# Two graph layers and a routed feed-forward: the gate computed inside the second layer, and lots gathered from lists in place of a scatter

## The chip, the cores and the metric

One core of one Trainium2 chip. The metric is the device time of one execution in microseconds (us), the median of several runs. Engines are called as in the profile: PE (TensorE), DVE (VectorE), ACT (ScalarE), POOL (GpSimd), SP (SyncE); "SPq" or "ACTq" is an engine's own sequencer, which issues its DMAs.

## What is computed

6250 nodes with 256 features (49 tiles of 128 rows), 100,000 edges of 8 types whose destinations are crowded at low node numbers.

```python
def rgcn(x, W, Wroot, b):          # W: 8 x 256 x 256
    seg = dst * 8 + etype
    mean = segment_sum(x[src], seg) / max(count(seg), 1)
    return x @ Wroot + b + einsum('nrd,rde->ne', mean, W)

x = x + rgcn(relu(rgcn(layernorm(x), ...)), ...)
z = layernorm(x)
top_w, top_i = top_k(z @ Wg + bg, 2)         # 8 experts, 2 for each node
w = softmax(top_w)
for e in range(8):                 # hidden width 1024
    out += w[:, e] * (gelu(z @ W1[e] + b1[e]) @ W2[e] + b2[e])
return x + out
```

## The kernel before, in words

The program is written engine by engine, with explicit semaphores; nothing is reordered by a tool. It has four stages.

**Setup** sorts edges, normalises x and writes a gather table to DRAM.

**Layers 1 and 2** run over the 49 tiles in the order of `RUNS`, in which runs of tiles with many edges (0 to 12) stand between runs with few. Edge rows come in 792 gathers per layer, each an indirect DMA of 128 rows on POOL (L509) into a ring of 16 slots; SP counts landings and frees slots (L395, L399). A tile is four "couples" (`couple` on PE, k = 0 to 3 in the three `tile_work`). In each, PE multiplies 0/1 selections made by DVE (L1036, and L1044 for every further block) with ring rows (L1384, L1385), ACT and DVE split the means in a high and a low half (L683, L1079), PE turns them (L1400) and, one or two tiles later, makes the 54 products of a tile (L1408). DVE adds the result to `acc` two tiles later (L1053; in layer 1 it is L1050), and takes its statistics (`bn_stats`, L1096). Layer 1 instead counts and inverts in each couple (L1066, L1069) and adds a bias (L1090) and a low half (L1057) in each tile. Layer 2 also reads expert weights for their maximum (ACT loads, L671, DVE L1102).

**The gate stage** begins when all tiles are in `acc`. DVE finishes the statistics of all 49 tiles and normalises tile after tile (`z_rows`, L1155); PE transposes each in f32 (`z_transposes`, L1484), ACT copies it (L745), PE multiplies by the gate matrix (`gate`, L1493). For each chunk of 7 tiles DVE picks the two experts (`choose`, L1169 to L1192), PE ranks (`ranks`, L1499 and L1500), DVE turns ranks into places (`place_rows`), and POOL scatters each tile's rows twice, once per chosen expert, into regions of `lot_in` in DRAM (L533, 98 indirect DMAs of 128 rows). `prepare` converts the weights of an expert (ACT L726, DVE L1217) for experts 0 and 1 inside this stage. At the end DVE works out how many lots each expert has, SP writes zero rows behind each region (L435), waits for all scatters, and loads the first lot (`load_lot`, L441).

**The lots.** A lot is 256 rows of one expert; there are 53. PE multiplies (L1535 up, L1545 down) and transposes the next lot (L1519), ACT applies GELU (L760), DVE splits and combines (`lot`, `take_lot`, `old_tags`, `lot_tags`). POOL gathers the old output rows (`fetch_old`, L545) and scatters the new (`store_new`, L552), then waits until they landed (`landed`, L557).

## Time and profile before

| | before |
|---|---|
| median of 3 runs | 2932.98 us (2931.1 to 2933.84) |
| the profiled execution, first to last instruction | 3487.9 us |
| PE busy | 2472.0 us (71%) |
| DVE, ACT, POOL busy | 1780.8, 1225.2, 1862.5 us |
| DMA | 333.24 MB, mean 96 GB/s |

The profile is of one execution with the hardware profiler on; its span is the only time of that execution that there is. In a row of a group of instructions, "busy, mean ns | idle before, releaser" are the summed time, the mean of one, and the idle time of the engine just ahead of them with what ended it. PE ends are modelled, so a matmul's own duration is longer than the step from one to the next.

### The profile page before, as it was taken

What the parts mean: (1) busy time and instruction counts of PE and PEld (TensorE: products, weight loads), DVE (VectorE), ACT (ScalarE), POOL (GpSimd) and SP (SyncE); (2) the same over time, 40 slices, a digit from 0 to 9 for tenths busy, and PEclk for the clock granted to TensorE, in tenths of its full rate; (3) what the DMA queues carried; (4) which work ended last, traced back from release to release, by engine and by line L of the source; (5) the groups of instructions that cost most, each with busy time, mean ns of one, the idle gap of its engine ahead of it and who ended that gap; (6) DMA issues with size and microseconds to landing.
All of it is one profiled execution on the core that took longest, in us unless ns stands there. A gap on an engine that the chain in (4) does not pass through costs nothing.

```text
span 3487.9 us, 82172 instructions
## 1 busy us (share of the span) xinstructions
PE 2472.0 (71%) x19212; PEld 1832.7 (53%) x19213; DVE 1780.8 (51%) x4984; ACT 1225.2 (35%) x2344; POOL 1862.5 (53%) x1980
## 2 busy tenths in 40 slices
PE   1346787678687786346776587687877428999999
PEld 0113565356365564114564365465656327888887
DVE  7324455345355454124454354354545338787777
ACT  5202343134243342012343143152432126555554
POOL 1666566655655554666556656655563543333333
PEclk9557999589799898557998798798997559999999
DMA  6223323233332232223333333333335234322222
GB/s 216 80 83 112 88 87 91 85 87 89 87 88 87 86 89 64 86 84 97 98 104 97 94 100 99 94 105 95 101 100 163 102 115 132 96 73 71 71 70 59
DMA packets 165489, 333.24 MB, mean 96 GB/s; under 512 B 36078, under 2 KB 102346, under 8 KB 165288
## 3 DMA queue, kind: packets, MB, share of 16 engines
q0 software_dynamic: 91632, 247.48, 24.1%
q1 hardware_dynamic: 39912, 41.03, 4.0%
q10 hardware_dynamic: 33872, 43.92, 3.9%
q8 instruction: 26, 0.43, 0.0%
q14 instruction: 47, 0.39, 0.0%
HBM read 285.39 MB, written 49.07 MB: 96 GB/s over the span
## 4 chain that ended last, share of the span: by engine, by line
PE 44%; issue 22%; DVE 10%; another core or an unknown queue 9%; DVEq 7%; SPq 2%; ACT 2%; DMA 1%; ACTq 0%; POOLq 0%; POOL 0%
PE more_banks L1408 13%; PE sum_banks L1384 9%; PE sum_banks L1385 7%; PE more_banks L1535 4%; PE sum_banks L1535 3%; PE more_banks L1400 3%; PE sum_banks L1545 3%; DVEq L1044 3%; DVEq L1041 2%; DVE sels L1044 2%; DVEq L1027 1%; DVE stage L1079 1%; DVE sels L1036 1%; PE sum_banks L1426 1%
## 5 line engine op out<-in xcount | busy, mean ns | idle before, releaser
L509 POOL DMA_INDIRECT ring<-table,tabs x1584 | 1526.9, 964 | 1046.4 <-SPq L399 670.0
L1384 PE MATMUL sum_banks<-ring,sels 128*128 x2348 | 726.6, 311 | 630.1 <-issue 420.1
L1408 PE MATMUL more_banks<-weights,stage 128*128 128x256 f16 x5292 | 919.1, 290 | 22.0 <-issue 21.4
L1385 PE MATMUL sum_banks<-ring,sels 128*128 x2348 | 732.2, 313 | 41.5 <-issue 38.7
L1384 PEld LDWEIGHTS sum_banks<-ring,sels 128*128 128x128 f16 (+1 forms) x2348 | 242.4, 103 | 928.2 <-issue 896.9
L683 ACT ACTIVATE stage<-sum_banks,inv 128x256 f16<-128x256 f32 x784 | 328.1, 473 | 789.5 <-issue 384.9
L1408 PEld LDWEIGHTS more_banks<-weights,stage 128*128 128x128 f16 x5292 | 531.1, 104 | 135.3 <-issue 37.1
L1036 DVE SCALAR_TENSOR_TENSOR sels<-lane,win_off,tabs 128x256 f16<-128x256 f16 x792 | 349.4, 482 | 422.1 <-remote 181.9
L654 ACT ACTIVATE stage<-more_banks 128x1024 f16<-128x1024 f16 x392 | 402.0, 1026 | 419.1 <-remote 405.6
L1044 DVE TENSOR_SCALAR sels<-lane,win_off,tabs 128x128 f16 x780 | 260.6, 334 | 495.8 <-issue 339.6
L1079 DVE SCALAR_TENSOR_TENSOR stage<-sum_banks,inv,stage 128x256 f16<-128x256 f32 x784 | 347.0, 479 | 57.2 <-issue 40.2
L1385 PEld LDWEIGHTS sum_banks<-ring,sels 128*128 128x128 f16 (+1 forms) x2348 | 241.9, 103 | 116.5 <-issue 68.0
L1400 PE MATMUL more_banks<-ident,stage 128*128 128x128 f16 x3136 | 272.3, 233 | 33.5 <-issue 21.9
L552 POOL DMA_INDIRECT out<-edge_work,lot_ids x106 | 109.2, 1030 | 332.3 <-DVE edge_work L1305 316.2
L681 ACT ACTIVATE stage<-sum_banks 128x256 f16<-128x256 f32 x196 | 75.2, 384 | 546.3 <-issue 231.2
L1400 PEld LDWEIGHTS more_banks<-ident,stage 128*128 128x128 f16 x3136 | 226.3, 105 | 69.9 <-issue 38.2
L1066 DVE TENSOR_SCALAR inv<-sum_banks 128x2 f32 (+1 forms) x196 | 31.1, 159 | 389.3 <-remote 150.1
L1545 PE MATMUL sum_banks<-weights,edge_work 128*128 128x256 f16 x1824 | 208.2, 275 | 8.9 <-DVE edge_work L1289 8.9
L760 ACT ACTIVATE stage<-sum_banks,edge_work,undo 128x256 f32<-128x256 f32 x212 | 117.2, 562 | 239.9 <-PE sum_banks L1535 211.2
L1545 PEld LDWEIGHTS sum_banks<-weights,edge_work 128*128 128x128 f16 x1824 | 179.4, 99 | 31.5 <-issue 9.8
L545 POOL DMA_INDIRECT edge_work<-out,old_ids x106 | 111.4, 1051 | 86.8 <-issue 77.6
L1287 DVE TENSOR_SCALAR edge_work<-stage,scales 128x256 f16<-128x256 f32 x212 | 75.5, 356 | 109.4 <-issue 59.9
(319 smaller groups left out, 2407.5 us busy)
## 6 DMA issues: line engine op xcount, KB each, us to landing
ring<-table,tabs POOLq DMA_INDIRECT x1584
weights<-L_ffn_W ACTq DMA_DIRECT2D x96, 178.5 KB
stage<-L_ffn_W ACTq DMA_DIRECT2D x16, 1024.0 KB, 5.0
edge_work<-lot_in SPq DMA_DIRECT2D x54, 260.0 KB
table<-edge_work ACTq DMA_DIRECT2D x49, 128.0 KB
lot_in<-sels SPq DMA_DIRECT2D x8, 260.0 KB
weights<-L_gnn_W SPq DMA_DIRECT2D x2, 1024.0 KB, 8.3
weights<-L_gnn_W ACTq DMA_DIRECT2D x2, 1024.0 KB
```

Source lines behind the costliest of these rows:

```text
L509: pool.indirect_dma_start(ring_rows[:, b % RING, 0:2 * D], None, tables[layer], bass.IndirectOffsetOnAxis(row_tab[:, b:b + 1], 0)).then_in ...
L654: act.activation(means[:, par, :, :, 2 * k * WIN:(2 * k + 2) * WIN].rearrange("p q r (v n) -> p v (q r) n", v=2), ps_turn[slot].rearrange( ...
L683: act.activation(mean16[:, slot, h, 0:D], ps_sum[slot][h][:, 0:D], ACT.Copy, scale=inv[:, ds(c * 2 + h, 1)]).then_inc(mean_high[layer], 1)
L1036: return v.scalar_tensor_tensor(sel[:, slot, h], lane16[:].unsqueeze(1).to_broadcast([P, 2, P]), win_off[:, ds(w, 1)], key_tab[:, ds((need ...
L1044: v.tensor_scalar(flat(sel_more[:, ds(block & (RING - 1), 1), :]), lane16[:], win_off[:, ds(w, 1)], key_tab[:, ds(block, 1)], ALU.add, ALU ...
L1079: v.scalar_tensor_tensor(mean16[:, slot, h, D:2 * D], ps_sum[slot][h][:, 0:D], inv[:, ds(c * 2 + h, 1)], mean16[:, slot, h, 0:D], ALU.mult ...
L1384: pe.matmul(to[:, 0:D + 1], hot, ring_row[:, ds(at + D, D + 1)], start=first, stop=last, skip_group_check=True)
L1385: return pe.matmul(to[:, 0:D], hot, ring_row[:, ds(at, D)], start=False, stop=last, skip_group_check=True)
L1400: out = [pe.transpose(ps_turn[slot][:, (4 * h + q) * P:(4 * h + q + 1) * P], mean16[:, slot, h, q * P:(q + 1) * P], ident16[:]) for h in r ...
L1408: return [pe.matmul(ps_out[par], rows[:, xp * KD + k, :], w16[:, wp, k, r * D:(r + 1) * D], start=part == PART_ORDER[0] and n == 0, stop=p ...
L1535: ins = pe.matmul(hid_bank[c % 4], up_sb[slot][:, wp, k, c * P:(c + 1) * P], lotT[:, zp, k, :], start=k == 0 and (wp, zp) == PART_PAIRS[0] ...
L1545: ins = pe.matmul(bank[2 + h][:, 0:D], hidT[:, hp, c, h * P:(h + 1) * P], down_sb[slot][:, wp, c, :], start=c == 0 and (hp, wp) == PART_PA ...
```

## The change

**In layer 2** (`gate_tiles` in place of `graph_tiles`: tiles 0 to 3 written out, then the loop by two). After a tile is in `acc`, DVE finishes its statistics by itself (`row_stats`, six small operations); ACT takes the root (`deviation`), DVE inverts (`z_row` on DVE, two operations), ACT normalises the tile into `z_rows` (`z_row` on ACT) and stores it to `z_dram`; a tile later PE transposes it (`z_transposes`, at the start of couple 0), ACT copies (`z_columns`), PE multiplies by the gate (`gate`, at the start of couple 2), and DVE adds the gate's bias (`logit_row`, between the two low halves of couple 2). The last four tiles (`EARLY` = 45 and on) get this behind the layer.

**In the gate stage** `choose` runs once for 45 tiles and once for 4. The scatter is gone. Each of the 12,500 rows has a rank in its expert; its low 7 bits (`low`) and its column 8*(rank // 128) + expert (`high`) become 0/1 rows (`pick_places`, DVE, 14 row sets a chunk), ACT and POOL scale the low ones by the row number in the tile and by the tile's number (`scale_part`, `low_tile`), and 28 f16 matmuls a chunk (`list_rows`) add up, for each place, which node it holds. DVE turns the sums into two tables of row numbers, POOL packs them (16 copies).

**In the lots** POOL gathers each lot's rows from `z_dram` by such a list (`gather_lot`) in place of SP's plain load, and copies the row numbers for its three pairs of indirect DMAs (`take_ids`); DVE's `old_tags` is gone. Zero rows behind the regions and `lot_in` are gone. SP stores `acc` to `out` up to tile position 44 already at the end of the layer. `prepare(1)` stands behind the lists. The core of the diff:

```diff
+                def row_stats(u):
+                    v.wait_ge(layer_done, u + 1)
+                    v.bn_stats(...).then_inc(bn_done, 1)
+                    v.wait_ge(bn_done, u + (TILES + 1))
+                    v.tensor_tensor(flat(mv[:, ds(u, 1), :]), ...)
+                    v.tensor_tensor(apart, ...).then_inc(mean_ready, 1)
+                    v.wait_ge(mean_ready, u * 2 + 1)
+                    v.tensor_scalar(mean, mean, 0.5, None, ALU.mult)
+                    v.scalar_tensor_tensor(apart, ...).then_inc(mean_ready, 1)
+                    v.wait_ge(mean_ready, u * 2 + 2)
+                    v.scalar_tensor_tensor(spread, ...).then_inc(var_ready, 1)
...
-                            if k == 3 and age == 2:
-                                v.wait_ge(layer_done, t - 1)
-                                v.bn_stats(flat(bn[:, ds(t - 2, 1), :]), flat(acc[:, ds(t - 2, 1), :])).then_inc(bn_done, 1)
+                            if k == 1 and age >= 3:
+                                z_row(t - 3, 1 - par, age >= 4)
+                            if k == 3 and age >= 2:
+                                row_stats(t - 2)
...
+                            if k == 0 and age >= 3:
+                                deviation(t - 3)
+                            if k == 0 and age >= 4:
+                                z_columns(t - 4, par, 1 - par)
+                            if k == 2 and age >= 3:
+                                z_row(t - 3, 1 - par, age >= 4)
...
+                    if layer == 1 and k == 0 and age >= 4:
+                        z_transposes(t - 4, par, 1 - par, t - 2)
                     regs, at, need, end = load_couple(c)
+                    if layer == 1 and k == 2 and age >= 4:
+                        gate(t - 4, par, ps_sum[slot][1][:, GATE_AT:GATE_AT + X])
...
-            for c in range(CHUNKS):
-                pool.wait_ge(zs_ready, c + 1)
-                for i in range(CHUNK):
...
-                    for k in range(2):
-                        pool.indirect_dma_start(lot_in, ...)
+            for c in range(CHUNKS):
+                pool.wait_ge(places_marked, 2 * c + 1)
+                if c >= 2:
+                    pool.wait_ge(listed, c - 1)
+                pool.tensor_tensor(low_tile[c % 2]..., low_hot[c % 2]..., node_tile..., ALU.mult).then_inc(tile_scaled, 1)
...
+            def pick_places(c):
+                if c >= 2:
+                    v.wait_ge(listed, c - 1)
+                    v.wait_ge(part_scaled, c - 1)
+                    v.wait_ge(tile_scaled, c - 1)
...
+                v.scalar_tensor_tensor(low_hot[c % 2], lane16..., 0.0, low, ALU.add, ALU.is_equal).then_inc(places_marked, 1)
+                v.scalar_tensor_tensor(high_hot(c), col_no..., 0.0, high, ALU.add, ALU.is_equal).then_inc(places_marked, 1)
...
-                sp.dma_start(lot_rows, lot_in[ds(row, LOT), :].rearrange("(h p) d -> p h d", p=P)).then_inc(lot_loaded, 16)
+                for h in range(HALVES):
+                    pool.indirect_dma_start(lot_rows[:, h, :], None, z_dram, bass.IndirectOffsetOnAxis(next_ids[:, h:h + 1], 0)).then_inc(lot_loaded, 16)
```

PE at a tile's end and the start of the next one in layer 2's loop (L1384 and L1385, now L1555 and L1556, multiply ring rows; L1408, now L1592, is a product). Before:

```order
L1400 MATMUL more_banks<-ident,stage 128x128 x8
L336 REGISTER_ALU
L336 COMPARE_AND_BRANCH
L1376 TENSOR_LOAD pe_row
L1433 REGISTER_ALU
L1384 ISA
L1384 MATMUL sum_banks<-ring,sels 128x257
```

Now:

```order
L1584 MATMUL more_banks<-ident,stage 128x128 x8
L392 REGISTER_ALU
L392 COMPARE_AND_BRANCH
L1573 MATMUL more_banks<-ident,weights 128x128 x2
L1547 TENSOR_LOAD pe_row
L1621 REGISTER_ALU
L1555 ISA
L1555 MATMUL sum_banks<-ring,sels 128x257
```

The two f32 transposes of a normalised tile (`z_rows` lies in `weights`) stand ahead of couple 0's first sums, and two f32 gate products stand in the same way ahead of couple 2's.

DVE behind the last two additions to `acc`. Before (L1155 then normalises 14 tiles):

```order
L1143 BN_STATS stage<-acc 128x6 x2
L820 TENSOR_TENSOR mv<-stage 128x49
L821 TENSOR_TENSOR stage<-stage 128x49
L822 TENSOR_TENSOR mv<-stage 128x49
L823 TENSOR_TENSOR stage<-stage 128x49
```

Now, at the far end of the stage, with the last three chunks' places (L1352 low, L1354 high), the tables, and expert 1's `prepare`:

```order
L1369 SCALAR_TENSOR_TENSOR weights<-stage,scales,weights 128x512 x8
L1352 SCALAR_TENSOR_TENSOR sels<-lane,edge_work 128x1792
L1354 SCALAR_TENSOR_TENSOR ring<-sels,edge_work 128x3920
L1352 SCALAR_TENSOR_TENSOR stage<-lane,edge_work 128x1792
L1354 SCALAR_TENSOR_TENSOR edge_work<-sels,edge_work 128x4704
L1352 SCALAR_TENSOR_TENSOR sels<-lane,edge_work 128x1792
L1354 SCALAR_TENSOR_TENSOR ring<-sels,edge_work 128x5488
L1430 TENSOR_SCALAR edge_work<-more_banks 128x400
L1431 TENSOR_SCALAR edge_work<-more_banks 128x400
L1432 SCALAR_TENSOR_TENSOR edge_work<-more_banks,edge_work 128x400
```

The 49 normalisations left DVE, and 14 wide operations, of 1792 and of 784 to 5488 elements, came to it.

POOL in the loop over an expert's lots. Before:

```order
L566 ISA
L552 DMA out<-edge_work,lot_ids 6250x256 x2
L542 ISA
L545 DMA edge_work<-out,old_ids 128x256 x2
L556 ISA
```

Now:

```order
L639 ISA
L593 ISA
L593 COPY next_ids<-edge_work 128x2
L594 ISA
L600 DMA edge_work<-z_dram,next_ids 128x260 x2
L593 ISA
L593 COPY out_ids<-edge_work 128x2
L594 REGISTER_ALU
L622 REGISTER_ALU
L625 DMA out<-edge_work,out_ids 6250x256 x2
L593 ISA
L593 COPY old_ids<-edge_work 128x2
```

The gather for the lot after the next and its copy stand ahead of the store.

## Rows read from the trace of the kernel before

**Rows 1.** Stretches: start:end, us; busy PE, PEld, DVE, ACT, POOL; PEclk, DMA, GB/s

```profile
112.00:1387.00 1275.00, 897.78 (x6762) 620.71 (x6762) 590.16 (x1726) 399.40 (x736) 748.10 (x777) 0.82 0.30 87
1387.00:2665.00 1278.00, 893.50 (x6760) 620.37 (x6760) 550.06 (x1369) 385.97 (x687) 764.25 (x798) 0.83 0.33 96
2665.00:2862.00 197.00, 71.19 (x330) 64.88 (x330) 76.41 (x320) 32.38 (x77) 99.43 (x108) 0.51 0.43 144
2862.00:3488.00 626.00, 594.11 (x5299) 518.17 (x5296) 476.88 (x1320) 336.50 (x736) 220.62 (x212) 0.98 0.27 81
2481.00:2551.00 70.00, 64.32 (x628) 53.65 (x626) 42.93 (x105) 38.89 (x72) 40.57 (x43) 1.00 0.38 108
```

**Rows 2.** DVE's tile results in layers 1 and 2: durations, first and last start

```profile
L1050 DVE SCALAR_TENSOR_TENSOR stage<-more_banks,gnn_undo,bias_bc x49: 472/475/484, 336.6 to 1382.7; 128x256 f32 x47, 128x256 f32<-128x256 f32 x2
L1053 DVE SCALAR_TENSOR_TENSOR acc<-more_banks,gnn_undo,acc x49: 473/475/485, 1626.8 to 2664.9; 128x256 f32 x46, 128x256 f32<-128x256 f32 x3
```

**Rows 3.** Gate stage, PE in order of time: start, duration

```profile
2664.84 0.27 PE L1479 MATMUL more_banks<-ident,edge_work 64*128 64x64 f32 x1
...
2672.34 0.67 PE L1484 MATMUL more_banks<-ident,ring 128*128 128x128 f32 x2
2672.80 0.86 PE L1493 MATMUL sum_banks<-edge_work,sels 128*128 128x8 f32 x4
2673.51 0.67 PE L1484 MATMUL more_banks<-ident,ring 128*128 128x128 f32 x2
...
2725.03 1.02 PE L1493 MATMUL sum_banks<-edge_work,sels 128*128 128x8 f32 x4 [9.69 <-issue]
...
2858.74 1.12 PE L1519 MATMUL more_banks<-ident,edge_work 128*128 128x128 f32 x4 [34.18 <-DMA edge_work<-lot_in]
2861.45 0.82 PE L1535 MATMUL sum_banks<-edge_work,weights 128*128 128x256 f16 x3 [1.59 <-DVE edge_work L1269]
```

**Rows 4.** Gate stage, POOL's scatters in order of time: two neighbours

```profile
2791.83 0.97 POOL L533 DMA_INDIRECT lot_in<-ring,edge_work  x1 [0.30 <-issue]
2793.11 0.97 POOL L533 DMA_INDIRECT lot_in<-ring,edge_work  x1 [0.30 <-issue]
```

**Rows 5.** DVE lines: min/median/max ns, first and last start

```profile
L1217 DVE SCALAR_TENSOR_TENSOR weights<-stage,scales,weights x48: 740/743/752, 2752.0 to 3056.9; 128x512 f16<-128x512 f32 x48
L954 DVE SCALAR_TENSOR_TENSOR weights<-weights,gnn_scale x2: 5000/5006/5011, 257.1 to 1550.2; 128x4608 f16<-128x4608 f32 x2
```

**Rows 6.** DVE in order of time: the scan, the scales, the lots' numbers

```profile
95.48 1.78 DVE L996 TENSOR_TENSOR_SCAN stage<-ones,stage 1x784 f32<-1x784 f32 x1
...
2675.38 1.07 DVE L1222 TENSOR_REDUCE most<-edge_work 128x4 f32<-128x512 f32 x1 [0.99 <-DMA edge_work<-most_dram]
...
2832.05 0.16 DVE L1242 SCALAR_TENSOR_TENSOR edge_work<-expert_no,edge_work 128x8 f32<-128x8 f32 x1
...
2834.47 0.48 DVE L1256 MEMSET edge_work<- 128x512 f32 x1 [0.29 <-DVE lot_meta L1254]
```

**Rows 7.** Setup, PE in order of time: seven 392-column f16 matmuls

```profile
77.35 2.47 PE L1350 MATMUL more_banks<-weights,ones 112*128 112x392 f16 x7 [5.57 <-DVE weights L914]
```

**Rows 8.** Groups by line: a POOL memset, ACT's copy, DVE's smallest operation

```profile
L499 POOL MEMSET stage<- 128x784 f32 x1 | 0.8, 757 | 20.5 <-DVEq L894 20.5
L745 ACT ACTIVATE sels<-more_banks 128x256 f32<-128x256 f32 x49 | 18.5, 382 | 104.8 <-remote 52.2 <-PE more_banks L1484 28.0 <-issue 19.9
L1066 DVE TENSOR_SCALAR inv<-sum_banks 128x2 f32 (+1 forms) x196 | 31.1, 159 | 389.3 <-remote 150.1
```

**Rows 9.** A lot in the last stage: POOL, then PE, each by time

```profile
3271.78 1.03 POOL L545 DMA_INDIRECT edge_work<-out,old_ids  x1 [0.30 <-DMA out<-edge_work,lot_ids]
3279.12 1.02 POOL L552 DMA_INDIRECT out<-edge_work,lot_ids  x1 [6.32 <-DVE edge_work L1305]
...
3270.68 0.60 PE L1519 MATMUL more_banks<-ident,edge_work 128*128 128x128 f32 x4
3271.12 5.40 PE L1545 MATMUL sum_banks<-weights,edge_work 128*128 128x256 f16 x48
```

675 lines of the change are left out of this document (419 added, 256 removed).

## The prediction

> **What bounds the kernel now.** I first cut the span at the three places where the work changes and read the stretches [rows 1]. Both layers take 1275 to 1278 us, the gate stage 197 us, the lots 626 us. In the lots PE works 594 of 626 us with a granted clock of 0.98: they are bound by PE. In the gate stage no engine is busy for more than half of the time (POOL 99 of 197 us, DVE 76, PE 71 at clock 0.51, the lower level of 1.2 GHz): it is a chain of waits. In order of time it runs from the end of layer 2 at 2664.8 to the first product of a lot at 2861.5, 196.6 us [rows 3]. POOL issues its scatters at best 1.28 us apart [rows 4], so 98 of them are 125 us. What lies around them is the lead to the first scatter, POOL's waits for places, the zero rows and the first load: PE waits 34.2 us for that load at the end.
>
> In layer 2 a stretch of five tiles with few edges takes 70 us, 14 us a tile, with PE busy 64.3 us at full clock, DVE 42.9 and ACT 38.9 [rows 1]. There PE is the bound. In tiles with many edges the mean is longer and PE idles, since POOL's gathers (764 of 1278 us busy) and their landings set the pace. DVE has room: from the first to the last tile result layer 1 takes 1046.1 us and layer 2 1038.1 us [rows 2], though DVE is busy for 40 us more in layer 1, 0.8 us a tile [rows 1], with a count and a reciprocal ahead of each couple's selections. Most of a microsecond of DVE time per tile thus costs next to nothing.
>
> **The gate stage, rebuilt from rows.** From here every time counts from the end of layer 2. DVE is the chain for the most part, so I add up its list. The unit: 512 elements take 0.743 us and 4608 take 5.006 us [rows 5], so an operation takes 0.21 us and 1.04 ns an element. The smallest is 0.16 us [rows 8], 0.25 with a link to the next.
> - The last-but-one tile's root stands on ACT behind a copy that waits for PE's transposes, which stand behind the layer's products: 1.5 us until DVE is free (0.46 for two transposes [rows 3], 0.38 for the copy [rows 8], the root and DVE's two operations).
> - `choose` for 45 tiles: 12 operations of 360 elements at 0.585 us, a scan of 400 at 1.78/784 us an element [rows 6], some small ones and the links: 10.1 us.
> - Last tile's result, statistics, maxima, `z_row`: 3.3 us. `place_rows` for 45 tiles: 4.9 us. `choose` and `place_rows` for 4 tiles, 23 small operations and a scan: 7.0 us. Logits and weights: 2.7 us.
> - Scales: 1.07 us and eight small ones, 2.4 us. The lots' numbers: 2.4 us (2832.05 to 2834.47) [rows 6]. `prepare(0)`: 8 x 0.67 = 5.4 us at the step of [rows 5].
> - `pick_places`: seven times 1792 elements at 2.08 us, and 784 to 5488 elements, 24.3 us: 38.9 us.
>
> That is 78.6 us of DVE. Behind it: the last 28 matmuls of 392 columns. Seven such take 2.47 us [rows 7], which is the step at the lower level of the clock, where this stage runs now [rows 1]: 9.9 us. Three DVE operations of 400 elements before the last table, 1.9 us. POOL's 16 copies of 50 numbers, 0.25 us each, 4.1 us with the first list (no row has such a copy; the ends are 0.1 and 1 us each, and the memset of 784 elements in 0.757 us [rows 8] is nearest). The first gather: two issues at 1.35 us and a landing of 2.2 us, 4.8 us. Transposes and `take_lot` up to the first product: 2.7 us (2858.74 to 2861.45) [rows 3]. The sum is 102 us. The trace has stalls in this stage that no dependency explains, one of 9.69 us on PE [rows 3]; straight code is as long as before, and I add one of 8 us. So 110 in place of 196.6: **minus 87 us** (ends: minus 105 without stalls and with the last matmuls at full clock; minus 50 with three stalls and copies of 1 us).
>
> What is free beside it: ACT's scaling of 1792 elements stands beside DVE's wide operations; the waits in `pick_places` from the third chunk on look two chunks back. Expert 0's weights are loaded from the moment the last tile is done and used 45 us later. `prepare(1)` (5.4 us) runs while POOL packs. The stores of `out` up to position 44 moved on SP from this stage to the end of layer 2, where nothing is queued behind them. The tags that SP writes to `z_dram` are needed only 50 us later.
>
> **Layer 2.** For 45 tiles PE gets two transposes and a gate product in two parts. In the gate stage a tile's step is 0.46 us from transposes to products and 0.71 us on to the next [rows 3], 1.17 us at the lower clock; four f32 transposes take 0.44 us at full clock in the lots (3270.68 to 3271.12) [rows 9]. So at full clock 0.22 and half of 0.71: 0.58 us a tile. 45 x 0.58 = **plus 26 us**. Tiles that wait for gathers hide theirs, which I leave as margin. DVE gets seven or eight small operations, about 1.7 us with their links; ACT a root, a copy of 0.38 us, a normalisation and a DMA issue, about 1.7 us. Against 14 us a tile that makes DVE 10.3 and ACT 9.5 us: hidden, as the two layers' equal pace shows [rows 2]. If the cover goes, it is because they stand in the chain of a couple (below). Ends: plus 10 and plus 90 us.
>
> **The lots.** PE's lot is unchanged, 626/53 = 11.8 us on the mean [rows 1]. POOL gets two more indirect DMAs and three copies, 3.5 us, in a queue that idles 6.3 us in each lot [rows 9]. The new gather stands ahead of the store but asks only for a lot that PE takes one and a half lots later. DVE loses three small operations. Zero, with ends of minus 5 and plus 20 us (one wait more at each of the 8 experts).
>
> **Sum:** 3487.9 - 87 + 26 = 3427 us for a profiled execution. The median of the timed runs is 2933 us, 555 us below that span. The lots cannot be what shrinks (PE is full there), and POOL's steps in the gate stage are long work of its own; the layers, with a register or branch instruction at every turn, are the likely place. So I carry the difference over unchanged: 2933 - 61 = **2872 us**. If the whole span shrank alike (0.84), it would be 2933 - 51 = 2882.
>
> **Rivals.**
> 1. *POOL and DVE block each other in the gate stage.* POOL's seven products of 1792 elements run exactly beside DVE's wide operations. If only one of them can run at a time, the products join DVE's chain. No row has a two-input operation on POOL. By the memset (0.97 ns an element, twice for two inputs [rows 8]) they are 7 x 3.4 = 24 us: 2872 + 24 = 2896. For it: nothing hides them then. Against it: no row shows a DVE operation stretched beside POOL's DMAs, though these do not read as much.
> The Trainium skill, page "SBUF — State Buffer", section "SBUF: two separate sides", says that the port pair that both use is "an exclusive lock, not a bandwidth split", for DVE operations with two SBUF inputs against a GpSimd operation that reads SBUF. That is this case, and speaks against the change; no run here shows it yet. The Trainium skill's "GPSIMD Engine Reference", section 3.1, has 4497 ns for a `tensor_tensor` of 2048 elements; as an estimate that is 3.9 us for 1792, so 27 us in place of 24.
> 2. *Couples wait for the new steps.* PE's gate product at couple 2 waits for ACT's copy, which stands behind the means and the root of couple 0; DVE's couples 2 and 3 now carry result, maxima, logits and statistics in a row. If a tile loses 1.6 us instead of 0.58: plus 72 instead of 26, 2918.
> 3. *The same to a full degree, and slower than before.* If each tile loses the time of most of a couple (14/4 = 3.5 us), say 2.5 us, the cost is 45 x 2.5 = 112 us: 2933 - 87 + 112 = 2958. It decides from 87/45 = 1.9 us a tile. Against it: DVE and ACT have a third of the time free, and every hand-over is one to two couples ahead of its use.
> 4. *Layer 2 hides PE's part too* because the timed execution is nearer to POOL's pace (792 gathers at the step of [rows 4] are 1014 us, against 1278) than the profiled one: 2846.
> 5. *The change does not do what it says*, in that lists still end late: POOL's copies or the first gather wait for the tags or for `z_dram`. Priced within the end of minus 50: 2909.
>
> **How the numbers follow.** The forecast has a chance of 0.42, rival 1 0.2, rival 2 0.13, rival 3 0.08, rival 4 0.1, rival 5 0.07. The likeliest gives 2872. The range: from rival 4 less some margin for the sum, 2835, to beyond rival 2, 2930; rival 3 and a little on each side are left out. A measurement of this kernel can tell about 0.2% from no change, 6 us. Below 2927 lie all cases but rival 3 and the upper edge of rival 2: faster 0.87, within 0.2% 0.04, slower 0.09.
>
> **What would show it right or wrong.** Right: the stretch from the last product of layer 2 to the first of a lot is about 110 us, DVE is busy in most of it, with L1352 at 2.1 us and L1354 from 1.0 to 5.9 us; light tiles take 14.6 us with PE still full; POOL idles some 3 us in each lot. Wrong: DVE rows stretched or late behind POOL's L576 (rival 1); PE waiting in front of L1579 or L1573, or light tiles above 15.5 us (rivals 2 and 3); PE waiting at lots for the gather.

## The result and the profile after

The changed kernel takes 3134.05 us (median of 4 runs, 3131.12 to 3140.09), the kernel before 2933.41 us (2931.1 to 2936.35): a ratio of 1.0685, 95% interval 1.067 to 1.07. It is 201 us slower; forecast were 61 us less.

One thing must be known before the traces are compared. The execution that the prediction was read from spans 3487.9 us; a second profile of the same, unchanged kernel spans 2930.4 us, like its timed runs, and the changed kernel's spans 3133.2. I therefore compare with the second profile. That the first one's excess is no property of the kernel is what the run before_again was for:

> The kernel before, unchanged, for a profile that can be laid beside the one after: that one's span is within 0.1% of its timed median, while the first profile of the kernel before is 555 us above its own. Theory A: the excess lay in POOL's gathers of the tiles with many edges, in both layers alike; this profile then has a span of about 2933 us, the heaviest tile takes about 46 us in place of 70, and light tiles stay at 14 us. Theory B: the excess is part of every profile of this kernel; then the span is 3488 us again.

Measured: 2933.21 us, ratio 1.0001 (0.9991 to 1.0011). The span of 2930.4 us is theory A's; its account of where the excess lay holds only in part. The heaviest tile takes 46.2 us in layer 1, as expected, but 57.4 in layer 2; tiles with few edges did not stay at 14 us but take 12.2 in layer 2; and of the excess of 557 us, some 50 lie ahead of layer 1's first result, 50 between the two layers, 36 in the gate stage and 12 in the lots, next to 407 in the two layers.

The windows by stage of this second profile of before are, in this order, from 1200 us (between the two layers) to the last product of layer 2, the gate stage up to the first product of a lot, the lots, and five tiles with few edges. The columns are busy time of each engine, granted clock, DMA share, GB/s:

```profile
core 0: us, PE busy (x) PEld busy (x) DVE busy (x) ACT busy (x) POOL busy (x), PEclk, DMA share, GB/s
1200.00:2156.00 956.00, 791.44 (x6661) 584.54 (x6659) 531.14 (x1322) 375.56 (x687) 718.91 (x747) 0.91 0.41 121
2156.00:2316.00 160.00, 67.52 (x328) 65.06 (x327) 76.61 (x319) 32.49 (x77) 98.55 (x108) 0.52 0.54 181
2316.00:2930.40 614.40, 588.01 (x5300) 519.17 (x5300) 478.32 (x1321) 325.52 (x736) 219.46 (x212) 0.98 0.27 82
2003.09:2064.19 61.10, 60.54 (x620) 52.84 (x619) 42.29 (x103) 37.98 (x71) 46.47 (x49) 1.00 0.45 132
```

The same three stretches of the changed kernel, columns as above:

```profile
1200.00:2289.50 1089.50, 848.81 (x6934) 635.29 (x6934) 578.06 (x1703) 417.95 (x827) 717.53 (x762) 0.88 0.41 119
2289.50:2416.10 126.60, 42.60 (x236) 28.38 (x235) 88.52 (x140) 28.18 (x36) 54.30 (x27) 0.60 0.23 62
2416.10:3133.20 717.10, 613.28 (x5300) 529.06 (x5300) 474.03 (x1161) 325.05 (x736) 362.08 (x476) 0.96 0.24 72
```

| from .. to | before, us | after, us | difference | forecast |
|---|---|---|---|---|
| first tile result to last product of layer 2 | 1325.0 to 2155.8: 830.8 | 1326.2 to 2289.4: 963.2 | +132.4 | +26 |
| gate stage | 160.2 | 126.7 | -33.5 | -87 |
| lots | 614.4 | 717.1 | +102.7 | 0 |

With the 1.2 us at the start that is +202.8, the difference of the two spans. The gate stage did get shorter. Both stretches around it, which I had taken as nearly free, got longer by over 100 us each. From the page of after, the busy times and one of the two queues that fetch instructions:

```profile
PE 2375.4 (76%) x19390; PEld 1800.6 (57%) x19391; DVE 1836.6 (59%) x5025; ACT 1229.7 (39%) x2443; POOL 1961.9 (63%) x2177
...
q14 instruction: 153, 1.25, 0.1%
```

and the same lines of the second profile of before:

```profile
PE 2318.1 (79%) x19212; PEld 1775.9 (61%) x19213; DVE 1782.6 (61%) x4984; ACT 1192.1 (41%) x2344; POOL 1865.3 (64%) x1980
...
q14 instruction: 47, 0.39, 0.0%
```

PE and VectorE are busy for only 57 and 54 us more, so most of the 202 us are waits on them. POOL is busy for 97 us more, and in the lots for 143 (362.1 against 219.5, last rows of the windows). The other line to see is that of queue q14, which fetches code: 153 packets of 8 KB in place of 47.

**Layer 2.** From result to result, tiles with few edges alternate between 14 to 17 and 19 to 22 us. The five that end between 2105.6 and 2191.2 take 85.6 us; the same five take 61.1 in before (the last row of its windows above), 12.2 each. VectorE between two of them:

```profile
2069.83 0.42 DVE L1194 BATCH_NORM_STATS2 stage<-acc  x1
...
2071.16 0.16 DVE L1204 SCALAR_TENSOR_TENSOR mv<-stage,mv  x1
2076.28 0.49 DVE L1169 SCALAR_TENSOR_TENSOR sels<-lane,win_off,tabs 128x256 f16<-128x256 f16 x1 [4.97 <-issue]
```

After the last small operation of a tile it does nothing for 4.97 us and waits for nobody ("issue"), at the point where its loop of two tiles jumps back. The DMA queues in the stretch 2072 to 2079 us show code arriving just then:

```profile
q14 instruction: 3, 0.02, 1.0%
```

Not all of the 4.97 us is the wait for code. VectorE's own sequencer takes the branch at the jump back (L392) at 2071.3 us and its next instruction at 2074.3:

```profile
L392 DVEq COMPARE_BRANCH  x1: 72/72/72, 2071.3 to 2071.3; - x1
L392 DVEq FUSED_REGOPS  x1: 105/105/105, 2074.3 to 2074.3; - x1
```

That step out of the branch takes 2.98 us at the median of the 21 jumps back, and 0.28 in code_moved_40 below, which executes the same loop. The other 1.9 us are a register load and address work, which stand at every tile's start.

Over the layer, the waits of VectorE for "issue" and of PE for VectorE:

```profile
DVE sels L1169 <- issue: 150.1, 57, 5.5
...
PE sum_banks L1555 <- DVE sels L1177: 102.4, 66, 5.3
```

and in before:

```profile
DVE sels L1036 <- issue: 14.4, 16, 1.5
```

where PE waits for VectorE (L1384 for L1044) for 60.0 us, 81 times.

**The lots.** Most lots take 12.7 to 13.2 us, in before 10.9. PE waits for the gathered rows 48 times:

```profile
PE more_banks L1714 <- DMA edge_work<-z_dram,next_ids: 87.8, 48, 4.5
```

One round of POOL in after, all its records:

```profile
2708.21 0.18 POOL L593 COPY next_ids<-edge_work 128x2 int32 x1 [2.58 <-issue]
2709.24 0.96 POOL L600 DMA_INDIRECT edge_work<-z_dram,next_ids  x1 [0.85 <-POOL next_ids L593]
2710.51 0.99 POOL L600 DMA_INDIRECT edge_work<-z_dram,next_ids  x1 [0.31 <-issue]
2711.51 0.19 POOL L593 COPY out_ids<-edge_work 128x2 int32 x1
2712.71 1.02 POOL L625 DMA_INDIRECT out<-edge_work,out_ids  x1 [1.01 <-issue]
2714.04 1.00 POOL L625 DMA_INDIRECT out<-edge_work,out_ids  x1 [0.30 <-issue]
2715.02 0.22 POOL L593 COPY old_ids<-edge_work 128x2 int32 x1
2716.10 0.98 POOL L618 DMA_INDIRECT edge_work<-out,old_ids  x1 [0.86 <-POOL old_ids L593]
2717.39 0.98 POOL L618 DMA_INDIRECT edge_work<-out,old_ids  x1 [0.30 <-issue]
2720.97 0.18 POOL L593 COPY next_ids<-edge_work 128x2 int32 x1 [2.61 <-issue]
```

and in before, where POOL's idle time [rows 9] is also 5.94 us a lot:

```profile
2707.29 1.01 POOL L552 DMA_INDIRECT out<-edge_work,lot_ids  x1 [5.94 <-DVE edge_work L1305]
2708.61 1.00 POOL L552 DMA_INDIRECT out<-edge_work,lot_ids  x1 [0.31 <-issue]
2709.91 1.04 POOL L545 DMA_INDIRECT edge_work<-out,old_ids  x1 [0.31 <-issue]
2711.26 1.02 POOL L545 DMA_INDIRECT edge_work<-out,old_ids  x1 [0.30 <-DMA out<-edge_work,lot_ids]
2718.22 1.01 POOL L552 DMA_INDIRECT out<-edge_work,lot_ids  x1 [5.94 <-DVE edge_work L1305]
```

In after POOL waits for no other engine in the whole round. It lasts 2708.21 to 2720.97 = 12.76 us, and that is the lot's length.

**The gate stage.** Of POOL's seven products the first two and the last three, in the timeline of POOL:

```profile
2311.75 3.83 POOL L576 TENSOR_TENSOR edge_work<-sels 128x1792 f16<-128x1792 f16 x1 [27.48 <-DVE sels L1352]
2323.35 4.66 POOL L576 TENSOR_TENSOR edge_work<-stage,sels 128x1792 f16<-128x1792 f16 x1 [7.76 <-DVE stage L1352]
...
2357.47 14.01 POOL L576 TENSOR_TENSOR edge_work<-sels 128x1792 f16<-128x1792 f16 x1 [9.04 <-DVE sels L1352]
2371.44 3.17 POOL L576 TENSOR_TENSOR edge_work<-stage,sels 128x1792 f16<-128x1792 f16 x1
2379.70 8.74 POOL L576 TENSOR_TENSOR edge_work<-sels 128x1792 f16<-128x1792 f16 x1 [5.09 <-DVE sels L1352]
```

and six of VectorE's operations beside them:

```profile
2311.58 0.97 DVE L1354 SCALAR_TENSOR_TENSOR ring<-sels,edge_work 128x784 f16<-128x784 f16 x1
...
2312.69 2.94 DVE L1359 TENSOR_SCALAR edge_work<-edge_work 128x45 f32<-128x45 f32 x1
...
2325.45 2.58 DVE L1335 CAST edge_work<-edge_work 128x8 int32<-128x8 f32 x1
...
2357.31 4.23 DVE L1354 SCALAR_TENSOR_TENSOR ring<-sels,edge_work 128x3920 f16<-128x3920 f16 x1
2361.46 2.01 DVE L1352 SCALAR_TENSOR_TENSOR stage<-lane,edge_work 128x1792 f16<-128x1792 f16 x1
2363.39 5.05 DVE L1354 SCALAR_TENSOR_TENSOR edge_work<-sels,edge_work 128x4704 f16<-128x4704 f16 x1
```

L1354 ends 0.80 us after the first product has begun (2312.55 against 2311.75), and 3.83 - 0.80 = 3.0 us are left. For the second it is 4.66 - 1.61 = 3.0, for the third and fourth (5.48 and 6.29 us long) and for the last (8.74 - 5.71) the same 3.0. The fifth takes 14.01 us: until 2368.44 VectorE's three wide operations run back to back, and 3.0 us later it ends. The sixth runs with VectorE idle, in 3.17. The other way round, the addition of a constant to 45 elements takes 2.94 us and a cast of 8 elements 2.58 us, and both end as the product does; so do another such cast (2.95 us) and another addition (3.14 us).

### The profile page after: what moved, and what is told of

It is laid out like the page before. It is cut to its first block, busy times and chain, and to the rows that moved or that the text cites. A ratio compares the mean times of both kernels' runs of the same rounds, so it can differ in the third digit from the quotient of the medians.

```text
span 3133.2 us, 83695 instructions
## 1 busy us (share of the span) xinstructions
PE 2375.4 (76%) x19390; PEld 1800.6 (57%) x19391; DVE 1836.6 (59%) x5025; ACT 1229.7 (39%) x2443; POOL 1961.9 (63%) x2177
## 4 chain that ended last, share of the span: by engine, by line
issue 27%; PE 24%; POOL 22%; DVE 8%; DVEq 6%; DMA 6%; POOLq 4%; SPq 0%; ACT 0%; ACTq 0%
POOL ring L547 16%; PE more_banks L1592 9%; PE sum_banks L1555 6%; PE sum_banks L1556 4%; DMA ring<-table,tabs 3%; PE more_banks L1584 3%; DVEq L1160 3%; POOLq L631 3%; DMA out<-edge_work,out_ids 2%; POOL edge_work L600 2%; POOL out L625 2%; DVE stage L1241 1%; POOL edge_work L576 1%; DVE sels L1169 1%; DVEq L1177 1%
## 5 line engine op out<-in xcount | busy, mean ns | idle before, releaser
L1555 PE MATMUL sum_banks<-ring,sels 128*128 x2348 | 699.7, 299 | 422.9 <-DVE sels L1177 269.2
L1592 PE MATMUL more_banks<-weights,stage 128*128 128x256 f16 x5292 | 878.1, 281 | 0.6
L1556 PE MATMUL sum_banks<-ring,sels 128*128 x2348 | 704.5, 301 | 0.0
L1555 PEld LDWEIGHTS sum_banks<-ring,sels 128*128 128x128 f16 (+1 forms) x2348 | 235.2, 100 | 700.0 <-issue 672.6
L1592 PEld LDWEIGHTS more_banks<-weights,stage 128*128 128x128 f16 x5292 | 514.0, 101 | 100.7 <-issue 12.4
L1177 DVE TENSOR_SCALAR sels<-lane,win_off,tabs 128x128 f16 x780 | 267.5, 343 | 387.9 <-SPq L451 318.7
L1584 PE MATMUL more_banks<-ident,stage 128*128 128x128 f16 x3136 | 257.3, 229 | 37.9 <-DVE stage L1241 37.8
L1556 PEld LDWEIGHTS sum_banks<-ring,sels 128*128 128x128 f16 (+1 forms) x2348 | 235.6, 100 | 48.8 <-issue 3.1
L1740 PE MATMUL sum_banks<-weights,edge_work 128*128 128x256 f16 x1824 | 219.4, 284 | 0.0
L625 POOL DMA_INDIRECT out<-edge_work,out_ids x106 | 110.3, 1040 | 82.8 <-issue 57.6
L600 POOL DMA_INDIRECT edge_work<-z_dram,next_ids x108 | 111.4, 1032 | 62.7 <-POOL next_ids L593 46.2
```

Source lines behind the costliest of these rows:

```text
L600: pool.indirect_dma_start(lot_rows[:, h, :], None, z_dram, bass.IndirectOffsetOnAxis(next_ids[:, h:h + 1], 0)).then_inc(lot_loaded, 16)
L1177: v.tensor_scalar(flat(sel_more[:, ds(block & (RING - 1), 1), :]), lane16[:], win_off[:, ds(w, 1)], key_tab[:, ds(block, 1)], ALU.add, ALU ...
L1555: pe.matmul(to[:, 0:D + 1], hot, ring_row[:, ds(at + D, D + 1)], start=first, stop=last, skip_group_check=True)
L1556: return pe.matmul(to[:, 0:D], hot, ring_row[:, ds(at, D)], start=False, stop=last, skip_group_check=True)
L1584: out = [pe.transpose(ps_turn[slot][:, (4 * h + q) * P:(4 * h + q + 1) * P], mean16[:, slot, h, q * P:(q + 1) * P], ident16[:]) for h in r ...
L1592: return [pe.matmul(ps_out[par], rows[:, xp * KD + k, :], w16[:, wp, k, r * D:(r + 1) * D], start=part == PART_ORDER[0] and n == 0, stop=p ...
```

## The experiments

The times are medians; the ratio is to the kernel before on the same chip, with its 95% interval. "Layer", "gate" and "lots" are differences to the second profile of before in the three stretches of the table, read from each run's own profile.

| run | us | ratio (95%) | layer | gate | lots | code packets |
|---|---|---|---|---|---|---|
| after | 3134.05 | 1.0685 (1.067, 1.07) | +132.4 | -33.5 | +102.7 | 153 |
| one_tile_loop | 3054.96 | 1.0409 (1.0392, 1.0426) | +54.6 | -35.0 | +103.8 | 45 |
| ids_together | 3068.26 | 1.0457 (1.044, 1.0474) | +134.0 | -35.0 | +39.7 | 153 |
| both_mended | 2988.72 | 1.0187 (1.017, 1.0204) | +54.1 | -35.4 | +38.8 | 46 |
| before_unused_code | 2935.03 | 1.0004 (0.9995, 1.0014) | -0.7 | -0.3 | +3.1 | 48 |
| before_one_tile_loop | 2933.98 | 1.0001 (0.9992, 1.0011) | +0.4 | +0.3 | -0.4 | 46 |
| products_on_act | 3108.39 | 1.0599 (1.0581, 1.0617) | +131.2 | -54.9 | +95.2 | 154 |
| all_four | 2955.36 | 1.0077 (1.006, 1.0094) | +53.5 | -53.5 | +15.7 | 46 |
| code_moved_40 | 3031.32 | 1.0331 (1.0313, 1.0348) | +30.9 | -33.3 | +101.3 | 48 |
| code_moved_128 | 3126.97 | 1.0661 (1.0643, 1.0679) | +124.7 | -32.9 | +103.9 | 154 |
| before_unused_moved_90 | 2981.73 | 1.0164 (1.0147, 1.0181) | +47.8 | -1.2 | +1.3 | 159 |
| stats_spread | 2906.86 | 0.9911 (0.9895, 0.9928) | +10.8 | -54.9 | +13.6 | 46 |
| two_tiles_placed | 2905.51 | 0.9907 (0.9891, 0.9924) | +5.6 | -54.8 | +14.4 | 49 |

Two kernels that execute the same work as before, before_unused_code and before_one_tile_loop, differ from it by up to 3.1 us in a stage: so much lies within one profile's noise.

### Layer 2: the code of VectorE's loop

one_tile_loop takes one tile a turn:

```diff
-            with eng.Fori(2, PAIRS) as i:
-                body(i * 2, 0, 4)
-                body(i * 2 + 1, 1, 4)
+            with eng.Fori(4, TILES) as t:
+                body(t, t & 1, 4)
```

> The changed kernel, with VectorE's loop of layer 2 written with one tile a turn in place of two (the same instructions run, in the same order; some 170 in the loop in place of some 330). Theory A (the loop's code has become too long to stay with the engine, so each turn waits for code at the jump back, 5.0 us, and once more inside, up to 1.7 us): every second tile loses its extra 5 to 6 us, 22 turns, so 110 to 145 us less than 3134: 2990 to 3024 us, and the packets of the instruction queue fall from 153 to about 50. Theory B (the couples wait for the new steps, rivals 2 and 3 of the prediction): nothing changes, 3134 us within 10.

Measured: 79 us less, all of it in the layer, and the code packets are gone: theory A, though 31 us less than its lower end. The alternation is gone too; behind the first heavy tiles a tile with few edges now takes 14 to 17 us. Two controls on the kernel before followed. before_one_tile_loop writes its layer-2 loop in the same form:

> The kernel before, with VectorE's loop of layer 2 written with one tile a turn, as in one_tile_loop. It tells what that form costs by itself. Theory A (the form costs nothing, since the old loop of 298 instructions stayed with the engine): 2933 us within 6, and the 51 us that one_tile_loop's layer 2 is longer than the one before are all the price of the added steps. Theory B (a jump back at each tile costs 1 to 2 us of VectorE, which light tiles can't hide): 2933 + 20 to 45 us, and the added steps cost that much less.

Measured: no difference. before_unused_code puts unexecuted code into each tile of its loop:

```diff
                             if k == 3 and age == 2:
+                                with v.If(end[0] > 30000):
+                                    for _ in range(16):
+                                        v.memset(most[:, 3:4], 0.0)
                                 v.wait_ge(layer_done, t - 1)
```

> The kernel before, with 16 small instructions and a branch over them in each of the two tiles of VectorE's loop of layer 2: the branch always skips them, so what is executed grows by one untaken or taken branch a tile, and the loop's code from some 298 to some 334 instructions, which is its length in the changed kernel. Theory A (length of the loop's code): every second tile of layer 2 takes 5 us more, 22 turns: 2933 + 80 to 130 = 3013 to 3063 us, with about 150 packets on the instruction queue in place of 47. Theory B (executed work alone costs): 2933 to 2938 us and 47 packets.

Measured: 2935 us and 48 packets, a miss. Length alone is not it. I had also counted from a listing of the program; the compiled one has, without labels, 281 instructions in the loop of before (from the 977th on), 315 with the unused code, 321 in the changed kernel (from the 1208th on). That left two theories: a limit between 315 and 321, or the place of the loop's ends in blocks of code. The next three runs put code that is never executed ahead of the loop, which moves the loop and nothing else:

```diff
                 regs, need, end = load_meta(0, 4)
+                if layer == 1:
+                    with v.If(end[0] > 30000):
+                        for _ in range(38):
+                            v.memset(most[:, 3:4], 0.0)
```

> The changed kernel with 38 small instructions and a branch over them ahead of VectorE's loop of layer 2, never executed: the loop's 321 compiled instructions (labels not counted) begin at the 1247th in place of the 1208th. before_unused_code showed that 315 instructions from the 977th on cost nothing. Theory A (code is kept in blocks, and what counts is how many blocks the loop touches; both earlier results together leave only offsets at which a move by 40 brings the 321 into one block fewer): the stall of 5 us at the jump back goes in every turn, 3134 - 80 = 3054 us, and the instruction queue has about 50 packets. Theory B (it is the length, with a limit between 315 and 321, or another cause): 3134 us and some 150 packets.

Measured: 103 us less than the changed kernel, which executes the same work; the 39 added instructions are a branch and what it skips. Its instruction queue, and VectorE's waits over the layer:

```profile
q14 instruction: 48, 0.39, 0.0%
```

```profile
DVE sels L1169 <- issue: 86.9, 45, 2.3
```

> The same with 126 such instructions: the loop begins at the 1335th, 127 further than in the changed kernel. It tells the size of the blocks if theory A of code_moved_40 holds: with blocks of 128 instructions (one packet of 8 KB each) it lies as in the changed kernel, 3134 us and 150 packets; with blocks of 256 it touches one block fewer, 3054 us and 50 packets. Theory B: 3134 us.

```profile
q14 instruction: 154, 1.26, 0.1%
```

Measured: 7 us less than the changed kernel, with all its packets: blocks of 128 instructions, not of 256.

> The kernel before with the unexecuted code in its loop (315 instructions, which cost nothing from the 977th on), moved to begin at the 1066th. Theory A (blocks): for every offset that the earlier results leave it now touches one block more, so each of 22 turns waits some 4 us for code: 2934 + 80 = 3014 us and about 150 packets. Theory B (length alone): 2934 us and 48 packets.

```profile
q14 instruction: 159, 1.30, 0.1%
```

Measured: 48 us more than the kernel before, and as many packets as in the changed kernel. The same 315 instructions cost nothing from the 977th on and 48 us from the 1066th on. The price is lower than the 80 us forecast, though VectorE's longest wait is again 5.0 us. VectorE has more room in that layer, which would fit, but that was not tested.

All six two-tile loops of these runs (and the 322 instructions of two_tiles_placed, below) fit one rule, which is inferred from them and not seen directly. A loop that touches three blocks of 128 compiled instructions stays with the engine; one that touches four is fetched again at each turn (106 packets of 8 KB more in 22 turns, about 5 a turn). code_moved_40 and before_unused_moved_90 were forecast from blocks before they ran, and code_moved_128 gave their size. One number is free in this: an unknown number of instructions stands ahead of the compiled ones. With any such number that is 47 to 71 more than a multiple of 128, the loops of 281, 315 (from the 977th) and 321 (from the 1247th) touch three blocks, and those of 321 (from the 1208th and the 1335th) and 315 (from the 1066th) four. The Trainium skill, "Runtime: NRT & Kernel Launch", section "Instruction fetch mechanics", says that a taken branch whose target isn't in the current two-page window, of 256 instructions a page, forces a DMA fetch before execution goes on. The traces agree with the fetch and show its price at the jump back, 2.7 us a turn (2.98 against 0.28). With the grain of 256 code_moved_128 disagrees: counted in pages of 256, no number of pages parts the seven loops rightly.

The 21 jumps back make 57 of the 101.5 us by which code_moved_40's layer is shorter than the changed kernel's. Most of the rest fits PE's clock. For the same matmuls PE is busy for 772.9 us of the layer at a mean granted clock of 0.91 in the changed kernel, and for 741.0 at 0.96 in code_moved_40, 32 us less. The five tiles with few edges of the changed kernel, columns as in the windows above:

```profile
2105.57:2191.15 85.58, 70.29 (x646) 59.86 (x644) 46.92 (x144) 42.87 (x86) 39.99 (x43) 0.90 0.34 95
```

In code_moved_40 PE is busy for 64.65 of their 69.77 us, at a clock of 1.00. In the changed kernel PE waits for VectorE three times in them, for 4.5, 4.0 and 4.4 us, and within 2 us of each wait's end the clock falls to its lower level of 1.2 GHz, for 3.4, 6.8 and 6.8 us. The last 12 us or so were not broken down.

### The lots: POOL's round

ids_together copies a lot's row numbers together (in outline; the counts of the waits follow):

```diff
-                        next_lot(start + j + 2, (start + j) * 3 + 4)
-                        store_new(start + j, (start + j) * 3 + 5)
-                        fetch_old(start + j + 1)
+                        pool.wait_ge(tags_taken, start + j + 2)
+                        copy_ids(next_ids, lot_rows_of, start + j + 2)
+                        copy_ids(out_ids, lot_outs_of, start + j)
+                        pool.wait_ge(packed, (start + j) * 3 + (5 + 2 * X + 1))
...
+                        store_new(start + j, None, True)
+                        fetch_old(start + j + 1, True)
                         landed(start + j)
```

> The changed kernel, with POOL's three copies of row numbers in a lot issued so that two of their three waits for a copy are gone or lie behind transfers; the transfers and their order are the same. Theory A (POOL is the bound of the lots: its own round of 6 indirect DMAs, 3 copies with a wait each and a drain is 12.75 us against PE's 11.33): the round falls by 1.7 us to 11.0, PE is the bound again, 45 lots lose 1.4 us: 3134 - 63 = 3071 us, and PE's waits ahead of the lot's transposes fall from 225 us to under 100. Theory B (PE waits for gathers that land late because of the traffic): the waits stay, 3134 us within 10.

Measured: 66 us less, 63 of it in the lots; a lot takes 11.4 us. Theory A. both_mended has both edits:

> Both edits above. If both of the A theories hold they add up, since they lie in different stages: 3134 - 125 - 63 = 2946 us, 2927 to 2965. If only one holds, about 3010 or 3071.

Measured: 145 us less than the changed kernel; the single gains were 79 and 66. The two causes are independent. What is left of 39 us in the lots pointed at POOL's round once more, 11.4 us against PE's 10.9. all_four drops the drain:

```diff
                 pool.sem_inc(res_free, 1)
-                pool.drain()
```

> The changed kernel with VectorE's one-tile loop, the row numbers copied together, no drain at the end of a lot on POOL, and the products on ScalarE. If what both_mended left in the lots (PE's round is 11.4 us against 10.9 before, 53 lots, 39 us in all) is still POOL's round, the drain's end takes it away: 2989 - 25 for the lots - 20 for the gate stage = 2944 us. If the wait that ends each lot is not the drain's but the landing of the store, the lots stay and it is 2969 us.

Measured: 33 us less than both_mended: 23 in the lots and 18 in the gate stage, of which some 4 are given back ahead of layer 2's first result. Of the 23 us, up to 7 may come with the products on ScalarE, as in products_on_act below, and not from the drain. It tells the two theories apart: the pause ahead of a round's first copy goes from 2.59 us (ids_together)

```profile
2710.89 0.19 POOL L616 COPY next_ids<-edge_work 128x2 int32 x1 [2.59 <-issue]
```

to 0.82 us (all_four), so 1.8 us of it were the drain's, and not the landing of the store:

```profile
2713.99 0.18 POOL L616 COPY next_ids<-edge_work 128x2 int32 x1 [0.82 <-DVE tags_next L1467]
```

### The gate stage: POOL's products against VectorE

products_on_act gives them to ScalarE:

```diff
-                pool.tensor_tensor(low_tile[c % 2].rearrange(...
-                                   node_tile[:, c * CHUNK:(c + 1) * CHUNK].unsqueeze(2).to_broadcast([P, CHUNK, 2 * P]), ALU.mult).then_inc(tile_scaled, 1)
+                for i in range(CHUNK):
+                    t = c * CHUNK + i
+                    ins = act.activation(low_tile[c % 2][:, 2 * i:2 * i + 2, :], low_hot[c % 2][:, 2 * i:2 * i + 2, :], ACT.Copy, scale=node_tile[:, t:t + 1])
+                ins.then_inc(tile_scaled, 1)
```

> The changed kernel, with POOL's seven products of 1792 elements in the gate stage made by ScalarE (7 x 7 scaled copies of 256 elements). Theory A (rival 1: POOL's product and VectorE's wide operations exclude each other; 2.9 us for each product, four of them in front of small VectorE operations, and the fifth held for 11 us): VectorE's casts and sums of 2.6 to 3.1 us fall to 0.2, its wait of 9.15 us for the fifth list goes, and the stage from the last product of the layer to the first of a lot falls from 126.7 to 100 to 110 us: 3134 - 20 = 3114 us. Theory B (PE's list products at the lower clock and ScalarE's own list set the pace): 3130 to 3140 us; ScalarE then is as late as POOL was.

Measured: the stage takes 105.3 us, 21.4 less, and the kernel 26 us less (7 us of that lie in the lots, unexplained). Theory A. ScalarE needs 2.88 us for a chunk, and VectorE's casts are back to 0.17 us:

```profile
2352.98 2.88 ACT L855 ACTIVATE edge_work<-sels 128x256 f16<-128x256 f16 x7
```

```profile
2325.15 0.17 DVE L1332 CAST edge_work<-edge_work 128x8 int32<-128x8 f32 x1
```

### A version that beats both kernels

stats_spread is all_four with two more edits, of which the first in outline:

```diff
                         if k == 2 and age >= 2:
                             sums_out(t - 2, par)
+                            if layer == 1:
+                                stats_row(t - 2)
...
                         for h in range(2):
+                            if late:
+                                (stats_scaled, stats_spread)[h](t - 2)
...
-                            if k == 3 and age >= 2:
-                                row_stats(t - 2)
```

> all_four with two more edits: VectorE's row statistics of layer 2 stand in couple 2 and between the operations of couple 3 instead of in a chain at the tile's border, and the first gather of the lots goes out ahead of the copies of the second list on POOL. Theory A (what the added steps cost in layer 2 is mostly VectorE's chain at the border, 1.5 us of statistics in front of 2.1 us of register work, with PE's own 0.6 us a tile as the floor): layer 2 falls by 20 to 28 us, and the gather first by 3: 2955 - 27 = 2928 us. Theory B (PE's added work and its hand-overs are the cost): the layer stays, 2952 us.

Measured: 2906.9 us, 0.9911 of the kernel before (0.9895 to 0.9928), 227 us less than the changed kernel. The layer fell from +53.5 to +10.8 us, more than forecast. The first gather's 3 us came as 1.4 in the gate stage. VectorE's waits over the layer show what went, its idle time at the border of a tile:

```profile
DVE sels L1189 <- issue: 38.7, 25, 1.8
```

PE's waits for gathered rows in the lots are down to

```profile
PE more_banks L1751 <- DMA edge_work<-z_dram,next_ids: 18.0, 5, 5.7
```

and 46 of the 53 steps from lot to lot take at most 12.0 us, nearly all of them 10.9; the long ones (up to 19.0 us) all lie among the first 17, as in before (up to 18.8 us).

> stats_spread with VectorE's loop of layer 2 in its two-tile form again, moved by unexecuted code so that it begins at the 1247th instruction (322 instructions), as in code_moved_40. Theory A (a jump back and its register work at each tile cost VectorE time that light tiles don't hide: code_moved_40 was 23 us shorter in the layer than one_tile_loop): the same 20 to 23 us come off 2907: 2885 us. Theory B (with the statistics off the border that time is hidden): 2907 us within 6.

Measured: 2905.5 us, so theory B: with the statistics off the border, the second jump back in two tiles is almost hidden (the layer is 5 us shorter, where 20 to 23 were forecast), and only the two together were a cost.

What is left in the layer is PE's. The five tiles with few edges take 66.3 us here, where before takes 61.1:

```profile
2013.77:2080.09 66.32, 65.19 (x650) 56.06 (x648) 46.52 (x143) 42.66 (x87) 49.61 (x52) 1.00 0.51 139
```

PE is busy for 65.19 of 66.32 us and waits for no other engine in them, so its added steps are paid in full there, about 1.0 us a tile. The layer as a whole is only 5.6 us longer than in before for another reason: its 34 steps from result to result at tiles with few edges are 20.9 us longer together, and the other twelve, tiles with many edges, are 15.2 us shorter. Why these got shorter was not tried.

## Why the prediction was wrong, step by step

**"What bounds the kernel now", the two layers' equal pace** [rows 2]. This failed as evidence. In the second profile layer 1 takes 845.7 us from first to last tile result (286.4 to 1132.1) and layer 2 831.1 (1325.0 to 2156.1), and the five tiles with few edges named above take 68.6 us in layer 1 against 61.1. So layer 1's light tiles, with 0.8 us more of VectorE each, are 1.5 us longer, in before already; that VectorE is the reason is likely and not shown. In the first profile both layers were slower throughout, so that totals told little. The sign was there to see: 555 us between the span and the median is a reason to distrust the rows of the layers, and I only used it to choose between two ways of scaling a sum.

**Layer 2, plus 26.** Measured plus 132.4. The failed step is "DVE 10.3 of 14 us: hidden". It put VectorE's added work at nothing, and it failed in two ways. The larger was in no rival: VectorE's longer loop was fetched again at each turn, which makes 101.5 us with what follows from it, PE's lower clock above all (963.2 - 861.7, code_moved_40). The smaller is VectorE's chain at a tile's border, which stood in front of some 2 us of register and branch work that the page doesn't count as busy (86.9 us in 45 waits in code_moved_40); with the statistics elsewhere and the code well placed the layer falls from +30.9 to +5.6 us.

Rival 3 came near the size, 112 us, by a wrong cause: no couple was lost in every tile, but 4.6 us on the mean in every turn of two tiles. Light tiles above 15.5 us, the sign I had given for rivals 2 and 3, came true and did not tell the causes apart; the alternation and the instruction queue did.

PE's own term was right in kind and too small. In two_tiles_placed a light tile is about 1.0 us longer, not 0.58: the two transposes take 0.33 us (forecast 0.22) and the gate product 0.44 (0.36), and the f16 transposes beside them get 0.3 us longer together. PE is full there, so rival 4, which hid this work, does not hold for light tiles. That the layer's sum is only +5.6 us comes from tiles with many edges getting shorter, which nothing in the prediction foresaw.

**The lots, zero.** Measured plus 102.7. The failed step is "3.5 us, in a queue that idles 6.3 us". The idle time was nearly right, 5.94 us. The added work wasn't: the round outside that idle time is 10.93 - 5.94 = 4.99 us in before and 12.76 in after, 7.8 us more. Two transfers with their gaps are 2.6 us; three copies are 0.6 us, but each is followed by a wait of 0.85 to 1.01 us before the transfer (less the 0.3 us that stood there anyway twice), and the drain and the loop's turn (2.6 us, of which 1.8 the drain) had always been there, hidden in the idle time. 4.99 + 7.8 is 1.8 us over PE's 10.9; 53 lots make 97 us. That the gather "asks only for a lot that PE takes one and a half lots later" was no help: a head start doesn't save a ring whose round is too long.

**The gate stage, minus 87.** Measured minus 33.5. 36 us of the gap are the base: the second profile has 160.2 us where the first had 196.6 [rows 1]. The new stage takes 126.7 us in place of my 110. Its wide operations came as summed: L1352 2.03 us (2.1), L1354 0.97 to 5.87 us (1.0 to 5.9), `prepare` 5.39 (5.4), `choose` 8.75 (10.1), the first list's operations 1.97 (1.9), the last list matmuls 7.5 (9.9). POOL's 16 copies took 8.5 us (4.1), the first gather 5.6 (4.8). The other step that failed is that rival 1 was left out of the sum: POOL's products and VectorE's wide operations were taken as running beside each other. It was priced at 24 us, and products_on_act measured 21.4. The Trainium skill's rule in "SBUF — State Buffer", section "SBUF: two separate sides", an exclusive lock and not a shared bandwidth, is what this trace shows. A product took 3.0 us where I had 3.4 from a memset; the estimate of 3.9 from the figure in the Trainium skill's "GPSIMD Engine Reference", section 3.1, was further off. Rival 1 deserved more than a chance of 0.2. Without the products the stage is 105 us; my sum before the 8 us for stalls was 102.

**The carried difference.** To lay a difference of two profiled spans on the median was right in form: the spans differ by 202.8 and the medians by 200.6 us. The numbers that went into it were not.

**The chances.** Slower had 0.09, nearly all of it from rival 3, whose cause did not come true. VectorE's steps in layer 2 and POOL's in the lots had been argued to be hidden by idle time that was not free, and I gave both arguments as if one profile had shown them.

## What to carry to other kernels

Idle time on a page is not room: in this kernel it held register, branch, drain and link time that the page does not count as busy. To see whether a queue can take more, write down its whole round from one record to its next return, with every wait for its own copies, and compare that with the round of the engine that sets the pace. When a change lengthens a loop on an engine, look at the code packets, not only at the operations, and if they rise, move or shorten the loop. And a profile whose span isn't that of the timed runs is to be taken again before its rows are used.

## What the runs showed of the hardware

- A loop's cost depends on where its code begins. 315 instructions on VectorE cost nothing at one place and 48 us at another, 89 instructions on; 321 cost 101 us more at one place than 39 further on. The fetch is about 5 packets of 8 KB a turn. From the branch back to the next instruction it is 2.98 us at the median, against 0.28 where the loop stays; with the register work of that place VectorE waits up to 5.5 us. PE's clock pays as well: 0.91 over the layer in place of 0.96, 32 us of PE's busy time.
- A product of two tensors on POOL and VectorE's wide operations exclude each other wholly: 3.2 us alone, 14.0 us behind 11 us of VectorE's. While it runs, VectorE's small casts and additions of a constant wait as well, 2.6 to 3.1 us for 0.2 us of work; one reduction (L1334) and two sums that read PSUM (L1332) took 0.2 to 0.3 us beside it.
- POOL's drain cost 1.8 us a lot: the pause ahead of a round's first copy was 2.59 us with it and 0.82 without.
- Left open: why products_on_act has 7 us less in the lots, why it and the kernels built on it reach layer 2's first result 3 to 5 us later (1329.5 to 1330.2 us in place of 1324.5 to 1326.9), why layers 1 and 2 take 1046 and 1038 us in the first profile [rows 2], in place of 846 and 831, and why tiles with many edges are shorter in two_tiles_placed than in before. None of this was tried.
